# A decoder layer's expert half on one Trainium2 core: other tile groups, a shorter first list, pads twice as dense

## The reference, cut to what matters

```python
combine = sum(one_hot(top_idx) * rw, axis=1)
for w_gu, w_d, ce in experts:
    g, u = split(x @ w_gu.T)
    out += (silu(g) * u) @ w_d.T * ce[:, None]
```

## Time and profile before

| what | us |
|---|---|
| median of 3 runs | 511.2 |
| lowest and highest run | 509.89, 515.54 |
| span of the profiled execution | 513.8 |

### The profile page before, as it was taken

How to read it: one execution, slowest core, us unless ns; L and a number is a source line. 1 busy time by engine, 2 the same in 40 slices (tenths; PEclk the granted TensorE clock), 3 DMA queues, 4 the chain that set the end, 5 groups by cost and what they waited for, 6 DMA issues and landing times.

```text
span 513.8 us, 12310 instructions
## 1 busy us (share of the span) xinstructions
PE 457.6 (89%) x3120; PEld 391.6 (76%) x3120; DVE 378.6 (74%) x1854; ACT 318.1 (62%) x869; POOL 327.8 (64%) x473
## 2 busy tenths in 40 slices
PE   3779999999999999999978999899999999989920
PEld 2567777887877787877756998799999999879910
DVE  4355688888778988777986886556565657998986
ACT  2367687777787777787736565556565656555520
POOL 4111347777677777777676777777766677756770
PEclk9989999999999999999999999999999999999985
DMA  7232535862323222321227669999655669999775
GB/s 199 81 130 74 166 118 180 229 193 93 107 91 105 105 87 93 104 93 75 74 86 242 201 232 295 315 292 290 218 158 143 204 197 339 357 307 318 262 259 190
DMA packets 52261, 93.79 MB, mean 183 GB/s; under 512 B 9974, under 2 KB 41246, under 8 KB 52002
## 3 DMA queue, kind: packets, MB, share of 16 engines
q1 hardware_dynamic: 37346, 46.11, 31.1%
q0 software_dynamic: 12240, 32.14, 16.7%
q10 hardware_dynamic: 2608, 14.76, 8.5%
HBM read 53.61 MB, written 43.41 MB: 189 GB/s over the span
## 4 chain that ended last, share of the span: by engine, by line
PE 47%; DVE 22%; DMA 9%; SPq 8%; issue 7%; ACT 5%; POOL 2%; POOLq 0%; DVEq 0%; ACTq 0%
PE bank L1411 9%; DVE NM L789 7%; PE bank L1443 6%; PE bank L1104 6%; DMA pool_a<-rows 4%; DVE NM L791 4%; PE bank L1245 4%; PE bank L1287 3%; PE bank L1362 3%; SPq L361 3%; SPq L366 3%; PE bank L1261 3%; PE bank L1166 2%; PE bank L1433 2%; PE bank L1099 2%
## 5 line engine op out<-in xcount | busy, mean ns | idle before, releaser
L469 POOL DMA_INDIRECT rows<-rowb,idx x112 | 110.9, 990 | 55.0 <-DVE rowb L889 28.3
L1411 PE MATMUL bank<-wgu_sb,PT 128*128 x572 | 105.0, 327 | 0.9 <-ACT PT L496 0.9
L1411 PEld LDWEIGHTS bank<-wgu_sb,PT 128*128 128x128 f32 x572 | 91.3, 190 | 1.0 <-issue 1.0
L479 POOL DMA_INDIRECT parts<-PT,dst_all x72 | 72.0, 1000 | 29.8 <-issue 22.6
L496 ACT ACTIVATE PT<-bank 128x512 f32<-128x512 f32 x108 | 61.6, 593 | 27.8 <-PE bank L1443 19.3
L1443 PE MATMUL bank<-wd_sb,VC 96*128 x286 | 73.6, 379 | 0.0
L589 ACT ACTIVATE PT<-bank 128x512 f32<-128x512 f32 x96 | 53.7, 619 | 5.7 <-PE bank L1261 5.7
L998 DVE SCALAR_TENSOR_TENSOR PT<-PT,bank 128x192 f32<-128x192 f32 x72 | 25.2, 349 | 41.1 <-ACT PT L623 41.0
L1443 PEld LDWEIGHTS bank<-wd_sb,VC 96*128 96x128 f32 x286 | 52.2, 190 | 4.0
L623 ACT ACTIVATE PT<-bank 128x192 f32<-128x192 f32 x72 | 23.7, 329 | 45.4 <-PE bank L1411 45.4
L496 ACT ACTIVATE Q<-bank 9x256 fp32r<-9x256 f32 (+1 forms) x96 | 42.5, 443 | 11.4 <-PE bank L1240 9.7
(11 more groups left out here) (270 smaller groups left out, 1142.8 us busy)
## 6 DMA issues: line engine op xcount, KB each, us to landing
pool_a<-rows SPq DMA_DIRECT2D x96, 148.5 KB
qN<-rows SPq DMA_DIRECT2D x47, 148.5 KB
wgu_sb<-wgu_d SPq DMA_DIRECT2D x8, 768.0 KB, 5.2
rows<-pad SPq DMA_DIRECT2D x33, 152.0 KB
pool_a<-parts ACTq DMA_DIRECT2D x5, 896.0 KB, 7.1
KA<-parts ACTq DMA_DIRECT2D x5, 896.0 KB
Q<-parts ACTq DMA_DIRECT2D x5, 896.0 KB
wd_sb<-wd_d SPq DMA_DIRECT2D x2, 1536.0 KB, 11.3
```

The costliest lines, as they stand in the source:

```text
L469: gp.indirect_dma_start(out=rows, out_offset=bass.IndirectOffsetOnAxis(ap=idx[b % 2][:, k:k + 1], axis=0), in_=rowb[b % 2][:, :], in_offse ...
L479: gp.indirect_dma_start(out=parts, out_offset=bass.IndirectOffsetOnAxis(ap=dst[q % NDST][:, j:j + 1], axis=0), in_=yb[q % FEED][:, j, :], ...
L1411: last = t.matmul(GU_PS[q % 2][:, j * 2 * NI:(j + 1) * 2 * NI], xTb[q % 2][:, j, k * P:(k + 1) * P], wgu_sb[:, k, one_of(expert[i]), :].sq ...
```

## The change

Five constants are changed, with two snapshots and one wait that follow from them, and the list of fetches at the end.

- `EPOCH` goes from (7, 12, 14, 15) to (5, 9, 12, 15), and `NA` from 56 to 40. `DONE`, which follows from them, goes from (44, 62, 69, 72) pairs to (37, 51, 62, 72), and the wait for pads and scatters from pair 28 to pair 20.
- `PADS`: a group of four pads behind each of the pairs 10 to 17, in place of one behind every second pair from 10 to 24.
- `FETCH`: before, tiles 0 to 7 at pairs 45, 47, ... 59, tiles 8 to 12 at 63, 64, 66, 67, 69, tiles 13 and 14 at 70 and 71. After, tiles 0 to 12 at 38, 40, 43, 45, 48, 50, 53, 55, 58, 60, 63, 65, 68. Tiles 13, 14 and 15 are then all in the last group and are fetched behind the last scatter's landing.
- The snapshot of tile 9 is taken, that of tile 14 no longer; the one of tile 12 fills two columns of `stack` in place of three.

```diff
-EPOCH = (7, 12, 14, 15)
+EPOCH = (5, 9, 12, 15)
-NA = 56
+NA = 40
-PADS = {q: range(4 * (q - 10) // 2, 4 * (q - 10) // 2 + 4) for q in range(10, 26, 2)}
+PADS = {q: range(4 * (q - 10), 4 * (q - 10) + 4) for q in range(10, 18)}
-FETCH = {**{45 + 2 * b: b for b in range(8)}, **{63 + 3 * b // 2: 8 + b for b in range(5)}, **{70 + b: 13 + b for b in range(2)}}
+FETCH = {38 + 5 * b // 2: b for b in range(13)}
...
             yc(NPAIR - 1)
-            fetch(FETCH[NPAIR - 1])
-            for b in range(NB - LASTS, NB):
-                fetch(b)
+            for b in range(NB):
+                if b not in FETCH.values():
+                    fetch(b)
...
-                        v.tensor_copy(stack[:, 2 * NE:].rearrange("p (k e) -> p k e", k=3), Msum[b % 2][:, :].unsqueeze(1).to_broadcast([P, 3, NE])).then_inc(S["snap"], 2)
+                        v.tensor_copy(stack[:, 3 * NE:].rearrange("p (k e) -> p k e", k=2), Msum[b % 2][:, :].unsqueeze(1).to_broadcast([P, 2, NE])).then_inc(S["snap"], 2)
...
-                pe.wait_ge(S["snap"], 3)
+                pe.wait_ge(S["snap"], 4)
```

## The result

The changed kernel takes 526.81 us (median of 4 runs, 522.51 to 527.56); the one before took 511.16 (4 runs, 509.89 to 515.54). The ratio is 1.026, with a 95% interval of 1.019 to 1.033: slower by 2.6%, clear of noise; whether it is more than 2% the interval leaves open. The medians alone give 1.031. Ratios leave out executions that were over 1.5% above the fastest of the same kernel, while the medians in this text are of all executions. The forecast was 523.5 us with a range of 517.5 to 530.

A forecast was written before the change was run, and what follows sets the result against it. It took PE as the bound, held up by SP's queue, late DVE sums and the end chain. 8.1 - 3.4 + 6.6 - 0.4 = 10.9 us gave 522.1 on the median, taken as 523.5 us; range 517.5 to 530.

The forecast's parts named there:

- stage A: Near 300 to 350 us, where pads are written: SP's queue, bound by its own issues, makes PE 8.1 us later.
- The pace: SP's queue with a group of pads behind each pair: 4.3 us a pair, where PE takes 2.83.
- pair 18's load: In SP's queue behind four more groups of pads at 2.6 us each: it moves by 10.4 us.
- The 3.9: Stage A: us taken from issue of the second half of pair 18's load until it is there, leaving 2.0 us slack.
- PE's idle time before the transposes of pairs 14 to 18: Sign in stage A's profile after the change: it adds up to 11 or 12 us, with none from 20 to 38.
- The wait for pads at pair 20: SP waits there for all pads to land: costs PE 0.3 us at a 5 us landing, some 3 at 8.
- Of the 4.0 us lost in stage B I take 3.4 as gone: Fetches every 2.5 pairs let DVE fit into PE's time and relieve the DMAs: a gain of 3.4 us.
- stage B: Near 421 to 486 us, where 12 fetches run beside the pairs; PE loses 4.0 us there before the change.
- Stage B is not relieved: Rival: the wait in front of the store is left, 3.4 us of gain stay out, 527 us; chance 0.13.
- three tiles at the end: Tiles 13, 14 and 15 are fetched and summed behind the last scatter's landing: 6.6 us more.
- the clock: Rival: PE idling in pairs 14 to 18 drops the clock to 1.2 GHz; four such pairs give 529 us; chance 0.08.
- The stretch at 264 us: Evidence for the clock rival: after 0.38 us busy of 2 us at 264 to 266, the clock fell to 1.2 GHz.

The follow-up runs named there:

- E1: The kernel before with only PADS changed: a group of four pads behind each of the pairs 10 to 17; 520.0 us, ratio 1.014.
- E4: The changed kernel with two tiny 32-byte DMAs more behind each of its eight groups of pads; 534.6 us, ratio 1.046.
- E7: The kernel before with only FETCH changed: tiles 0 to 7 every 2.5 pairs from pair 45, the rest at pairs 64 to 71; ratio 1.000.
- E9: The changed kernel with the fetches of tiles 0 to 12 at the places of the kernel before; 525.6 us, ratio 1.023.
- E6: The changed kernel fetching one of seven rows for tiles 0 to 12, with as many additions of the same size; ratio 1.013.
- E5: The changed kernel with four of DVE's five additions for tiles 0 to 12 cut to 8 columns, fetches and stores whole; ratio 1.014.
- E2: The kernel before with tiles 13, 14 and 15 in the last group and fetched behind the last landing; 517.6 us, ratio 1.0085.

## Why the prediction was right, and which of its steps were not

**Right: what happens in stage A, and its size.** SP's queue is bound by its own issues and PE starves behind it. E1 puts the pads at about 1.4% of the change's 2.6%, and E4 moves PE by SP's extra issue time without bytes. Two inner numbers were off and cancelled, which is luck. The pace was 4.55 us a pair, not 4.3, and counted from pair 0 the second half of pair 18's load went out 12.0 us later than before (59.32 against 47.35), not 10.4. Against that, this load was there at most 2.6 us after its second half's issue (334.87 to 337.50), not 3.9. The 3.9 was not wrong for every load: of those that PE stood waiting for, pairs 14 and 15 took 2.7 us, pair 16 took 3.8 (325.45 to 329.21) and pair 13 took 3.9 (311.48 to 315.41). PE's idle time before the transposes of pairs 14 to 18 adds up to some 7 us, not to the 11 or 12 that were to show it: the waits began at pair 12 (0.85 us, then 1.93 at pair 13), and at pair 17 the slow clock took the wait's place. The wait for pads at pair 20 cost nothing: they land in 2.6 us (median), and pairs 19 to 44 run at 2.83 us without a gap.

```profile
rows<-pad SPq DMA_DIRECT2D x32, 152.0 KB, 2.6
```

**Wrong: "Of the 4.0 us lost in stage B I take 3.4 as gone".** It lost 5.8, and the timing shows no gain from the fetches' places either (E7, E9). The step counted DVE's time (2.5 pairs and one tile in 6.7 us, against 7.06) as what held it, and took the DMAs' 37 GB/s off one full stretch of 333. DVE's room was at most a part of it: E6 shows that it can be 94% busy and hold nobody, as long as the rings have room, and E5 that with room made for DVE some of the loss stays. The rings were not freed. Moving a fetch does not remove its bytes, and the share still went to 1.00 at 346 GB/s from 460 to 480 us, where the kernel before had 0.99 at 333. The rival "Stage B is not relieved" described this; I had given it 0.13 and its sum of 527 is where the median came out.

**Mis-sized: three tiles at the end.** The term itself was near (6.2 us from landing to end, forecast 6.6). I left out that tiles 13 and 14, taken away from in front of the last landing, also leave the rings to the last scatters: its landing fell from 4.69 to 2.10 us. Net 2.7 us in this profile, 3.7 by the medians of the thirteen.

**A rival that came true in part and cost little: the clock.** It fell in the gap ahead of pair 16 (0.24 and 0.78 us busy in two windows of 2 us) and again behind pair 52, once in each stage and not for four pairs. In stage A PE had nothing else to do, so it cost about 1 us or less. In stage B it added 1.5 us to a gap of 3.1. That is the throttling that the Trainium skill describes (TensorE: Matmul & The Clock Gate, "HAM oscillation — how this bites in real kernels"); the trace agrees that a wait for DMA can set it off, here twice, but E1, E6 and E9 went through stage A's waits without a fall. The stretch at 264 us, which the prediction counts for the rule, was not a wait for DMA: PE stood 1.62 us there for DVE (line 789).

**The sum against the median.** By E1 and E2 the two parts give 1.014 x 1.0085 = 1.023, the whole 1.026 with an interval of 0.7% to both sides; the fetches' places add nothing that can be told. Stage B's missing gain and the end's smaller loss went opposite ways (5.2 us more and 3.5 us less than forecast in this profile), so that the total was near is in part luck. The forecast was 3.3 us low on the median. The span's difference (11.8) is smaller than that of the medians (15.7), because the profiled execution of the kernel before was, going by its span, the slowest of its four. Stage A varies too: with the old pads the profiles lost 3.9, 2.7 and 2.3 us up to pair 26. That executions differ mostly in stage B is likely from its losses of 1.4 to 8.6 us, but no profile of a faster execution of the kernel before shows it.

**Open.** Whether the earlier fetches cost or save one or two us in stage B: E9 and the spread of that stage don't allow a verdict. How much of the 10 us that E4's timing moved by, where its profile moved by 4, is the draw of the profiled executions. Whether pads issued from a second engine's queue would take stage A's loss away was not tried.

## What to carry to other kernels

Count the issues of the queue that feeds the bound engine as if they were its work: 32 pads of 0.5 us each cost little while the queue has a lead (from pair 19 to 25 the kernel before lost 0.6 us beside four groups of them), and nearly all of their time once it has none. An engine at 95% beside a ring at 100% is easily taken for the cause; cut the bytes and the work separately before moving either, and hold the result against how much the same kernel varies from one execution to the next. And when a transfer is moved away, look at what was landing beside it.

## What the runs showed of the hardware that was not expected

- The last scatter, one block, landed 2.10 to 2.11 us after its start in all six profiles with three tiles fetched last, with no fetch under way, and after 3.85 to 6.05 us in the seven with fetches of 896 KB beside it.
- The length of a gap does not say by itself whether the granted clock falls from 2.4 to 1.2 GHz. It fell at gaps of 3.37 and 3.15 us in the changed kernel, of 2.62 us in E5 (pair 14) and of 2.18 us in E4 (pair 50), and not at gaps of 2.82 and 3.00 us in E1 (pairs 14 and 16).
- The Trainium skill says that issuing from several engines only saves the sequencer's time, "usually small relative to the DMA itself" (DMA: Bandwidth & Descriptors, "Issuing engines are not separate DMA queues"). Each issue was small beside its DMA here too, 1.93 us for four pads of 152 KB against a median landing of 2.6 us for each. Yet these issues together were the bound, since they stood in one queue with the loads that PE waited for.
